# Adding the heads' results to the residual on VectorE, and a shorter shift

## The reference, cut to what matters

```python
hh  = h.reshape(n, H, D)
ft  = jnp.einsum('nhd,ed->nhe', hh, W_fc)
a1  = jnp.einsum('nhd,hd->nh', ft, attn_l)
a2  = jnp.einsum('nhd,hd->nh', ft, attn_r)
e   = jax.nn.leaky_relu(a1[src] + a2[dst], negative_slope=0.2)
m   = jax.ops.segment_max(e, dst, num_segments=n)
ee  = jnp.exp(e - m[dst])
agg = segment_sum(ee / segment_sum(ee, dst)[dst] * ft[src], dst)
res = jnp.einsum('nhd,ed->nhe', hh, W_res)
out = jax.nn.relu((res + agg).reshape(n, H * D))
```

## Time and profile before

| | us |
|---|---|
| median of 3 runs | 2479.14 (2478.87 to 2480.29) |
| the profiled execution | 2480.09, with a span of 2478.3 |

### The profile page before, as it was taken

The page is one execution under the profiler, slowest core; times in us unless marked ns, Lnnn a source line. Parts: engine busy times, 40 slices in busy tenths (PEclk is TensorE's granted clock), DMA queues, the critical chain, the costliest instruction groups (busy, mean ns, idle before and its releaser), DMA issues.

```text
span 2478.3 us, 29974 instructions
## 1 busy us (share of the span) xinstructions
PE 2173.8 (88%) x10953; PEld 1837.3 (74%) x10954; DVE 1228.3 (50%) x1882; ACT 780.9 (32%) x1062; POOL 451.2 (18%) x378
## 2 busy tenths in 40 slices
PE   3998761888888389999999999999999899999997
PEld 1555440333333179999999999999999899999997
DVE  7887656999995452233333342232333342344335
ACT  0133332888886231121221231121221231212212
POOL 0000001899999200000000000000000000000000
PEclk9999885999999589999999999999999999999999
DMA  0133332211110523333423423333323423335332
GB/s 17 42 86 88 89 91 59 89 32 32 32 32 16 159 90 88 99 90 105 121 83 114 113 71 89 97 106 110 117 77 108 123 66 103 121 102 139 100 99 78
DMA packets 138639, 215.04 MB, mean 87 GB/s; under 512 B 87580, under 2 KB 87818, under 8 KB 138513
## 3 DMA queue, kind: packets, MB, share of 16 engines
q1 hardware_dynamic: 99179, 147.28, 21.1%
q0 software_dynamic: 39344, 66.16, 9.3%
HBM read 182.38 MB, written 30.62 MB: 86 GB/s over the span
## 4 chain that ended last, share of the span: by engine, by line
PE 58%; DMA 5%; DVE 2%; ACT 2%; issue 0%; SPq 0%; ACTq 0%; DVEq 0%
PE banks L1101 30%; PE banks L1073 27%; DMA w_raw<-in_L_gnn_w_root_dram 3%; DVE w_lo L1342 1%; ACT w_hi L1221 1%; DMA s_x<-x_tiles 1%; PE banks L1136 1%; DMA emb_raw<-in_L_gnn_w_rel_dram 0%; PE banks L1110 0%; PE banks L1123 0%; PE banks L1154 0%; DVE h_lo L1373 0%; ACT accT L1249 0%; DVE tail_stats L1392 0%; DVE back L1390 0%
## 5 line engine op out<-in xcount | busy, mean ns | idle before, releaser
L1073 PE MATMUL banks<-ct_in,h_hi 125*128 125x416 f32 (+1 forms) x1710 | 604.5, 353 | 0.6 <-ACT accT L1206 0.6
L1073 PE MATMUL banks<-ct_in,h_lo 125*128 125x416 f32 (+1 forms) x1710 | 603.2, 353 | 0.0
L1101 PE MATMUL banks<-g_hi,w_hi 128*128 128x416 f32 (+1 forms) x1440 | 518.4, 360 | 21.6 <-DVE g_lo L1364 21.5
L1101 PE MATMUL banks<-g_lo,w_hi 128*128 128x416 f32 (+1 forms) x1440 | 513.7, 357 | 0.0
L1101 PE MATMUL banks<-g_hi,w_lo 128*128 128x416 f32 (+1 forms) x1440 | 513.4, 357 | 0.0
L1342 DVE TENSOR_TENSOR w_lo<-w_raw,w_hi 128x768 fp32r<-128x768 f32 (+1 forms) x228 | 227.9, 1000 | 468.2 <-ACT w_hi L1221 468.2
L1221 ACT CAST w_hi<-w_raw 128x768 fp32r<-128x768 f32 (+1 forms) x228 | 197.8, 868 | 449.8 <-PE banks L1101 354.6
L1073 PEld LDWEIGHTS banks<-ct_in,h_lo 125*128 125x128 f32 x1710 | 323.7, 189 | 4.4
L1073 PEld LDWEIGHTS banks<-ct_in,h_hi 125*128 125x128 f32 x1710 | 322.5, 189 | 4.1 <-ACT accT L1206 0.8
L1237 ACT CAST g_hi<-gs 128x416 fp32r<-128x416 f32 (+3 forms) x180 | 97.5, 542 | 702.7 <-DVE gs L1352 702.7
L849 PE MATMUL head_sums<-pw,x 125*65 125x512 f32 x720 | 273.0, 524 | 51.5 <-POOL pw L647 35.2
(11 more groups left out here) (189 smaller groups left out, 1538.5 us busy)
## 6 DMA issues: line engine op xcount, KB each, us to landing
w_raw<-in_L_gnn_w_rel_dram SPq DMA_DIRECT2D x117, 384.0 KB, 3.3
ct_in<-s_ct POOLq DMA_DIRECT2D x18, 2031.2 KB, 28.1
w_raw<-in_L_gnn_w_rel_dram SPq DMA_DIRECT2D x54, 448.0 KB, 3.9
ct_in<-s_ct POOLq DMA_DIRECT2D x9, 2041.0 KB, 28.4
s_ct<-ct_stage SPq DMA_DIRECT2D x30, 610.4 KB
w_raw<-in_L_gnn_w_root_dram SPq DMA_DIRECT2D x39, 384.0 KB, 3.2
w_raw<-in_L_gnn_w_root_dram SPq DMA_DIRECT2D x18, 448.0 KB, 5.8
low_spread<-s_low SPq DMA_DIRECT2D x12, 610.4 KB
```

The source lines that it names most:

```text
L1073: ins = nc.tensor.matmul(pb[0:rows, PA, 0:s.w], a, b, start=j == 0, stop=j == len(pairs) - 1)
L1101: ins = nc.tensor.matmul(pb[:, m, 0:s.w], a, b, start=s.first and j == 0, stop=s.last and j == len(parts) - 1)
```

## The change

Two parts.

The first: POOL's `add` is gone. DVE's product of sums and reciprocals now goes back to where it came from, in PSUM, and a second DVE instruction adds it to `res`, in the same place of the list, waiting for the first (`divided`). `shared`, for which PE's `spread`, `turn_sums` and one more product wait, is counted by the addition now and was counted by the multiplication.

The second: the shift has eight operations and had eleven. The two for nodes without an edge are left out, and the multiplication of `a2` by the slope is done once for all heads (`a2_low`, 125 x 10 x 12), in front of the first `lows`.

```diff
-GONE = 1e25
-        steps = sb("bias_steps", [T, 7, NT], F32)
+        steps = sb("bias_steps", [T, 5, NT], F32)
...
             def lows(h):
-                a2, at, n = a2_col[:, :, h], [steps[:, j] for j in range(7)], h * 8
+                a2, at, n = a2_col[:, :, h], [steps[:, j] for j in range(5)], h * 5
                 pool.wait_ge(maxed, (h + 1) * NT)
                 pool.wait_ge(low_ready, 3 * h)
                 nc.gpsimd.tensor_tensor(at[0], tops[:, h * NT:(h + 1) * NT], a2, ALU.add).then_inc(bias_step, 1)
-                nc.gpsimd.tensor_scalar(at[5], a2, SLOPE, None, ALU.mult).then_inc(bias_step, 1)
                 pool.wait_ge(bias_step, n + 1)
                 nc.gpsimd.tensor_scalar(at[1], at[0], 0.0, 1.0 - SLOPE, ALU.max, ALU.mult).then_inc(bias_step, 1)
                 nc.gpsimd.tensor_scalar(at[2], at[0], SLOPE, None, ALU.mult).then_inc(bias_step, 1)
+                pool.wait_ge(bias_step, n + 3)
+                nc.gpsimd.tensor_tensor(at[3], at[1], at[2], ALU.add).then_inc(bias_step, 1)
                 pool.wait_ge(bias_step, n + 4)
-                nc.gpsimd.tensor_tensor(at[3], at[1], at[2], ALU.add).then_inc(bias_step, 1)
-                nc.gpsimd.tensor_scalar(at[4], at[0], -GONE, None, ALU.is_gt).then_inc(bias_step, 1)
-                pool.wait_ge(bias_step, n + 6)
-                nc.gpsimd.tensor_tensor(at[3], at[3], at[4], ALU.mult).then_inc(bias_step, 1)
-                pool.wait_ge(bias_step, n + 7)
                 if h >= 2:
                     pool.wait_ge(low_turned, h - 1)
-                nc.gpsimd.tensor_tensor(at[6], a2, at[3], ALU.subtract).then_inc(bias_step, 1)
-                nc.gpsimd.tensor_tensor(lows_of[:, h % 2, 2], at[5], at[3], ALU.subtract).then_inc(low_ready, 1)
+                nc.gpsimd.tensor_tensor(at[4], a2, at[3], ALU.subtract).then_inc(bias_step, 1)
+                nc.gpsimd.tensor_tensor(lows_of[:, h % 2, 2], a2_low[:, :, h], at[3], ALU.subtract).then_inc(low_ready, 1)
...
-            def add(h):
-                pool.wait_ge(shared, h + 1)
-                if h == 0:
-                    pool.wait_ge(res_in, 16)
-                at = res[:, :, h * HD:(h + 1) * HD]
-                nc.gpsimd.tensor_tensor(at, share.rearrange("p m t f -> p (m t) f"), at, ALU.add).then_inc(res_added, 1)
...
+            nc.gpsimd.tensor_scalar(a2_low[:], a2_col[:], SLOPE, None, ALU.mult).then_inc(a2_scaled, 1)
+            pool.wait_ge(a2_scaled, 1)
             lows(0)
             lows(1)
...
-                dve.wait_ge(res_added, h)
-                nc.vector.tensor_tensor(share, sums[:, :, :, 0:HD],
-                                        rden[:, :, :, None].to_broadcast([T, 2, NT // 2, HD]), ALU.mult).then_inc(shared, 1)
+                nc.vector.tensor_tensor(sums[:, :, :, 0:HD], sums[:, :, :, 0:HD],
+                                        rden[:, :, :, None].to_broadcast([T, 2, NT // 2, HD]), ALU.mult).then_inc(divided, 1)
+                dve.wait_ge(divided, h + 1)
+                if h == 0:
+                    dve.wait_ge(res_in, 16)
+                at = res[:, :, h * HD:(h + 1) * HD].rearrange("p (m t) f -> p m t f", m=2)
+                nc.vector.tensor_tensor(at, sums[:, :, :, 0:HD], at, ALU.add).then_inc(shared, 1)
```

More of the change, by code:

```diff
@@ L501, with attention @@
 R1_SPANS = [(286, 512), (798, N - 798), (0, 286)]
-def attention(nc, io, dram, x, res, share, oT, cols, csum, csum16, nbr, y, stored, proj_out, rows_out, node, ident):
+def attention(nc, io, dram, x, res, a2_low, oT, cols, csum, csum16, nbr, y, stored, proj_out, rows_out, node, ident):
     a1_high, a1_low, a2_col, a_rows = cols
@@ L556, in attention @@
         o_kept = sem("o_kept"); o_turned = sem("o_turned"); denned = sem("denned"); shared = sem("shared")
-        res_added = sem("res_added")
+        divided = sem("divided"); a2_scaled = sem("a2_scaled")
         block = ctx.enter_context(nc.Block())
@@ L622, in lows @@
                 nc.gpsimd.tensor_scalar(at[2], at[0], SLOPE, None, ALU.mult).then_inc(bias_step, 1)
+                pool.wait_ge(bias_step, n + 3)
+                nc.gpsimd.tensor_tensor(at[3], at[1], at[2], ALU.add).then_inc(bias_step, 1)
                 pool.wait_ge(bias_step, n + 4)
-                nc.gpsimd.tensor_tensor(at[3], at[1], at[2], ALU.add).then_inc(bias_step, 1)
-                nc.gpsimd.tensor_scalar(at[4], at[0], -GONE, None, ALU.is_gt).then_inc(bias_step, 1)
-                pool.wait_ge(bias_step, n + 6)
-                nc.gpsimd.tensor_tensor(at[3], at[3], at[4], ALU.mult).then_inc(bias_step, 1)
-                pool.wait_ge(bias_step, n + 7)
                 if h >= 2:
                     pool.wait_ge(low_turned, h - 1)
-                nc.gpsimd.tensor_tensor(at[6], a2, at[3], ALU.subtract).then_inc(bias_step, 1)
-                nc.gpsimd.tensor_tensor(lows_of[:, h % 2, 2], at[5], at[3], ALU.subtract).then_inc(low_ready, 1)
-                pool.wait_ge(bias_step, n + 8)
+                nc.gpsimd.tensor_tensor(at[4], a2, at[3], ALU.subtract).then_inc(bias_step, 1)
+                nc.gpsimd.tensor_tensor(lows_of[:, h % 2, 2], a2_low[:, :, h], at[3], ALU.subtract).then_inc(low_ready, 1)
+                pool.wait_ge(bias_step, n + 5)
                 high = lows_of[:, h % 2, 0]
-                nc.gpsimd.tensor_copy(high.bitcast(F32R), at[6]).then_inc(low_ready, 1)
+                nc.gpsimd.tensor_copy(high.bitcast(F32R), at[4]).then_inc(low_ready, 1)
                 pool.wait_ge(low_ready, 3 * h + 2)
-                nc.gpsimd.tensor_tensor(lows_of[:, h % 2, 1], at[6], high, ALU.subtract).then_inc(low_ready, 1)
+                nc.gpsimd.tensor_tensor(lows_of[:, h % 2, 1], at[4], high, ALU.subtract).then_inc(low_ready, 1)
             def weights(u):
@@ L674, in _ @@
                     lows(h + 2)
-                if s == 3 and h >= 2:
-                    add(h - 2)
                 if s == 5 and h == H - 2:
                     kinds_and_zeros()
-            add(H - 2)
-            add(H - 1)
         @block.scalar
@@ L1486, in build @@
         with sb("x", [T, NT, D1], F32) as x_place:
-            share = x_place[:, :, D1 - HD:D1].rearrange("p (m t) f -> p m t f", m=2)
+            a2_low = x_place[:, :, D1 - H:D1]
             x = x_place[:, :, 0:H * (HD + 1)].rearrange("p t (h f) -> p t h f", f=HD + 1)
@@ L1493, in build @@
         h_lo = t("h_lo", [T, NT, D1], F32R)
-        attention(nc, io, dram, x, res, share, oT, (a1_high, a1_low, a2_col, a_rows), csum, csum16, nbr, y, stored, proj_out, rows_out, (hot, hot_rows, emb_cols, many), ident)
+        attention(nc, io, dram, x, res, a2_low, oT, (a1_high, a1_low, a2_col, a_rows), csum, csum16, nbr, y, stored, proj_out, rows_out, (hot, hot_rows, emb_cols, many), ident)
         ct0 = t("ct_in0", [T, NT, WIDE], F32R)
```

## The result

The changed kernel takes 2484.31 us (median of 20 runs) against 2480.34 for the kernel before on the same chips: a ratio of 1.0017, 95% interval 1.0010 to 1.0023. By that ratio it is slower by 4.2 us, 2.5 to 5.7. One of the 20 runs took 7554.96 us, and one of the kernel before beside e8 and e9 took 6609.52; both are left out of the ratios. The forecast was 2478.3 with a range up to 2483.0, and a chance of 0.86 for a difference within 0.2%. The difference is within 0.2%, but the time lies above the range, and the sign is wrong. The profiled execution after took 2483.13, its span 2481.2, which is 2.9 longer than the span before.

What follows compares the result with a forecast made beforehand. DVE's closed ring was taken to bound heads 3 to 9, POOL's list heads 10 and 11. Terms 3.9 - 0.6 - 0.5 - 3.7 + 0.1 = -0.8 us gave 2479.3 profiled, 2478.3 as median, range 2475.5 to 2483.

Steps and rivals of the forecast that it cites:

- the seam of 0.86: DVE, heads 2 to 9: from multiplication to next start grows from 0.74 to 1.60 us, +0.86 a head.
- 0.48 and 0.46 for the waits: DVE, middle heads: the wait before unit 0 falls from 0.78 to 0.48 us; that before the first maximum stays 0.46.
- the two heads on POOL with -3.7: Heads 10 and 11, where POOL sets the end: a shorter shift and two additions gone give -3.7 us.
- A: Rival, slower: the product written to PSUM goes over its elements twice, 6.5 us in all, 2484.8 us; chance 0.08.
- B: Rival, slower: POOL's `pw` holds DVE's addition, 2.1 us more at eight heads, 2495 us; chance 0.03.
- C: Rival, faster: POOL's ring holds DVE's, so DVE's addition disappears in idle time, 2472.3 us; chance 0.04.
- D: Rival, no visible change: ACT or PE takes POOL's place in heads 10 and 11; 2481.3 us if a fifth returns; chance 0.08.
- PE stands there 0.86 longer, and so does POOL behind it, but both have room then: Seam of heads 2 to 9: PE and POOL wait 0.86 us longer behind DVE's addition, counted as free room.
- POOL and PE then are ahead, so PE is free when DVE's last maximum arrives: Middle heads: POOL loses 2.24 us a head, so DVE's wait before unit 0 shrinks by 0.30.
- the handover: From head 10's first `bend_low` to POOL's last shift: 6.90 us becomes 6.4, -0.5.
- head 2: Its late first maximum covers the addition and the wait at its end falls from 1.14 to 0.48 us: -0.6.
- the tail: After the last `pw`: PE's second product waits for the addition, +0.86, the last addition is quicker on DVE, -0.75: +0.1 us.

Runs made afterwards that it cites:

- e8: The kernel before with only the shorter shift, POOL's addition kept, run again for a second profile: 2488.83 us, ratio 1.0038 to the kernel before.
- e9: The kernel with the shorter shift alone, plus a dense PE product of 320 columns before `spread_r1` of heads 3 to 10: 2479.30 us, ratio 0.9998 to the kernel before.
- e4: The changed kernel without any addition to the residual, the product still going back to PSUM: 2481.32 us, ratio 1.0008 to the kernel before.
- e6: The kernel with the shorter shift alone, plus a dense PE product of 256 columns before `spread_r1` of heads 3 to 10: 2477.88 us, 0.9992 of the kernel before.
- e5: The changed kernel plus a dense PE product of 125 rows and 512 columns before `spread_r1` of heads 3 to 10: 2481.21 us, 1.0007 of the kernel before.
- e3: The changed kernel with the first two products of `spread_r1` computed three times for heads 3 to 10: 2482.60 us, ratio 1.0013 to the kernel before.
- e7: The kernel before with four of the ten products of `turn_sums` computed twice: 2494.02 us, ratio 1.0062 to the kernel before.
- e1: The kernel before with only the shorter shift, POOL's addition kept: 2488.63 us, ratio 1.0037 to the kernel before.

## Why the prediction was wrong

Right, by its own steps: the seam of 0.86 (0.83 and 0.82, 0.86 apart), 0.48 and 0.46 for the waits, 31.24 for a head where 31.2 was forecast, the two heads on POOL with -3.7, the product written to PSUM at no extra cost (A: 0.83 against 0.82), no contention with `pw` (B: 0.82), no gain from a hidden addition (C), and no other engine that took POOL's place in heads 10 and 11 (D). The time of rival A, 2484.8, is close to the 2484.3 measured, but by chance: its mechanism did not occur.

The step that failed is "PE stands there 0.86 longer, and so does POOL behind it, but both have room then", and with it "POOL and PE then are ahead, so PE is free when DVE's last maximum arrives". I counted room on PE as free and had no term for its clock, which was at 1.00 in the earlier trace rows. In its place the runs showed that the clock fell at every middle seam, with the same gather at 4.37 in place of 2.27. Where the room was enough, at five seams, that cost nothing. Where it wasn't, DVE and POOL waited for PE. Of the 6.0 us that the attention stage ended later than forecast (+5.2 in place of -0.8), 3.3 are mostly two middle heads of 32.85 in place of 31.24, 2.2 the handover (8.58 in place of 6.4, POOL waiting 3.74 for a slow gather), 0.8 head 2 (1.66 in front of its first maximum, where I had thought the seam covered) and 0.3 the tail; the earlier start of unit 0 gives 0.6 back.

I had the sign to look for in front of me. At the seam of head 2 in the trace before, PE stood 0.46 for DVE's last maximum and the clock fell behind it:

```profile
484.61 0.39 PE L827 MATMUL spreads<-a_rows,pick_rows 2*125 2x286 f32 x1 [0.46 <-DVE tops L762]
...
487.51 3.61 PE L849 MATMUL head_sums<-pw,x 125*65 125x512 f32 x6
```

I took the 1.30 of the earlier trace rows as "PE is late" without asking why it was late only there.

That the clock's falls cost the time is shown: e4 takes DVE's addition away and the middle heads stay as long, e6 and e9 add work to PE alone and take 9.5 to 11 us off the kernel with the shorter shift. For the changed kernel itself e5 shows it in the middle heads (-2.95), and not in the whole time.

What exactly brings a fall is not settled. It isn't PE's stand for DVE alone: in e3 and e7 PE didn't stand and the clock fell, and in e1 and e8 it stood about as short at seams with a fall (0.23) as at one without (0.20). It isn't the length of the seam alone either, as e7 shows. In e1 and e6 to e9 some falls lie inside gathers just behind PE's stand of 2.0 for POOL at unit 4, so the seam is not the only place; the kernel before has the same stand in its middle heads (1.98 at 542.55) and no fall there. Why the dense product helps is therefore argued and not shown. The Trainium skill (TensorE: Matmul & The Clock Gate, section "HAM oscillation — how this bites in real kernels") tells of long idle gaps of PE as what brings the clock down. Here it fell with no idle gap over 1.2 us at the seam, and in e3 with no wait of PE in the rows of the seam, and where the two differ the measurement decides.

## What to carry to other kernels

Where several engines are nearly full, and PE is one of them, work taken off another engine can cost time, because PE's clock can fall where it had stayed up. Before such a change, look in the trace for the places where PE already fell to 1.2 GHz and what it did there, and price each place where PE would stand next to its small products as a possible slow stretch, not as free room. A dense product beside the small ones is worth a try: 0.5 us a head took 11 us off the kernel with the shorter shift, and gave nothing clear in the changed kernel.

## What the hardware showed that I had not expected

Taking three small operations out of POOL's list, 0.74 us a head, made the kernel 0.37% and 0.38% slower in two separate sets of runs (9.3 and 8.1 us between the medians), with every other engine's list unchanged. The same kernel differs from run to run: it took 2481.7 to 2494.4 in one set, and its two profiles, at 2481.7 and 2488.8, have 17 and 24 us at half clock in the middle heads.
